# Attention logits from stacks of 48 float32r rows, two heads in the halves of TensorE's rows

## The chip, the cores and the metric

One core of one Trainium2 chip. The metric is the device time of one execution in microseconds; less is better. The kernel is one launch that does everything.

## The reference, cut to what matters

`x` is 2 x 2048 x 256 (batch, tokens, features). A layer norm with modulation from a condition vector gives `h`; then causal attention with 16 heads of 16 features, an output projection and a gated residual; then a second modulated norm, a two-layer net of 1024 hidden units with routed low-rank terms, and a second gated residual. The part at issue is the attention:

```python
qkv = x @ W_qkv.T + b_qkv
q, k, v = (heads(t) for t in jnp.split(qkv, 3, axis=2))     # n, 16 heads, 2048, 16
logits = jnp.einsum('bhqd,bhkd->bhqk', q, k) / jnp.sqrt(jnp.float32(HEAD))
logits = jnp.where(causal[None, None], logits, -jnp.inf)
attn = jax.nn.softmax(logits, axis=-1)
o = jnp.einsum('bhqk,bhkd->bhqd', attn, v)
```

## The kernel before, in words

There are three stages after a short set-up, each a block that all engines leave together.

**Stage 2, the projections** (to about 134 us). Eight blocks of 512 tokens: VectorE normalises, TensorE transposes and projects to q, k, v with each float32 operand split into a float32r high and low part, three passes (`product`, line 358). ScalarE copies q and k out twice (line 499): in float32 and as the first bfloat16 part. VectorE takes the rest (line 565) and the second part (line 567), POOL the third part (line 527); POOL also splits the weights of the last stage (lines 518, 522). SyncE stores the three parts to DRAM as `qk_parts`, four DMAs a block (line 425). ScalarE may not start block n before the store of block n - 2 has landed.

**Stage 3, the attention** (about 134 to 1067 us). Work goes by group: 4 heads (`GH`) of one batch, 8 groups. For each group, `kst` and `qst` hold 6 stacked rows-of-16 per head, the products of parts that are kept (1-1, 1-2, 1-3, 2-1, 2-2, 3-1), so that one bfloat16 matmul over 96 rows gives logits of about float32 quality; 6 DMAs for q and 6 for k bring one block of 512 tokens (lines 616 to 632). There are two passes over the logits:

- The pass for the maxima (`event`, line 711): logits with queries on the partitions, at most 512 columns in one of three PSUM banks (4 to 6), the causal mask of the diagonal added by a matmul of `mask_q` with a bfloat16 identity (lines 729, 732). VectorE reduces each bank to its row maximum (line 862) and so gives the bank back. When the last unit of a query block J is reduced, VectorE makes three bfloat16 parts of minus the maximum (`make_parts`, lines 835 to 845), TensorE turns them (line 720), VectorE copies them to `mT` (line 850), and three DMAs put them into rows 96 to 98 of `qst`. Rows 96 to 98 of `kst` are ones (POOL's memset, line 925). There are 140 units and 4 turns a group, 144 events.
- The pass for the sum (`logits`, line 743, and `values`, line 763): per tile of 128 keys (40 a group), logits over 99 rows with keys on the partitions (lines 756, 760), two heads to two PSUM banks; ScalarE's Exp of both banks (line 816); then the product with v, four heads at once in four groups of 32 array columns, in float32 (line 772), two tiles late. The probabilities' sum comes from a column of ones.

TensorE's order is written out by hand (lines 781 to 790). The events of the pass for the maxima run ahead: the first `AHEAD` = 69 events of the next group lie in the current group's tiles, and before the first group they run alone (line 777).

```python
                for n in range(NKT):
                    logits(n, 0)
                    maxima(SLOTS_OF_TILE * n)
                    if n >= PV_LAG:
                        values(n - PV_LAG, s, c)
                    ...
                    maxima(SLOTS_OF_TILE * n + 1)
                    logits(n, 1)
                    maxima(SLOTS_OF_TILE * n + 2)
```

The waits that tie the engines: an event waits for the reduction three banks earlier (line 716), `logits` for the Exp of the same half a tile earlier (line 754), `values` for the Exp of its tile (line 766). The groups' steps run in a loop of two (`over_steps`, line 876). After the last step TensorE does 24 matmuls that nobody reads (`UNREAD[0]`, line 794).

**Stage 4** (from about 1068 us) is the projection of the attention's output and the net; the diff does not touch it.

## Time and profile before

| | |
|---|---|
| runs | 1407.65, 1411.41, 1412.89 us (median 1411.41) |
| the profiled execution | 1412.92 us, its span 1411.2 us |
| TensorE busy (matmuls) | 1300.2 us (92%) |
| TensorE weight loads | 693.9 us (49%), beside the matmuls |
| VectorE busy | 1032.8 us (73%) |
| ScalarE busy | 774.5 us (55%) |
| POOL busy | 172.8 us (12%) |
| mean granted TensorE clock | 0.954 |

PE is TensorE's matmul, PEld its weight load, DVE VectorE, ACT ScalarE, SPq SyncE's DMA queue. A matmul's listed time includes the way through the array, so neighbours overlap; the distance from one start to the next is what one costs in a dense row. A clock of 1.00 is 2.4 GHz, 0.50 is 1.2 GHz.

### The profile page before, as it was taken

The numbers are of one execution on the slowest core, as the hardware profiler recorded it, in microseconds if no ns is written. First come the engines' busy times: TensorE is split into PE (matmuls) and PEld (weight loads), VectorE is DVE, ScalarE is ACT, GpSimd is POOL, SyncE is SP. The second block draws the span as 40 slices with busy tenths as digits, with TensorE's granted clock in tenths as the row PEclk, the third lists the DMA queues.
The fourth block names the chain that finished last, engine by engine and source line by source line (L and its number), as shares of the span: only waits on it lengthen the run. The fifth ranks groups of instructions, "written<-read, shape, count | busy, mean of one in ns | idle before, by whom it ended". The sixth has DMA issues, their size and how long they took to land. (4 is left out here: it accounts for less than half of the span.)

```text
span 1411.2 us, 26070 instructions
## 1 busy us (share of the span) xinstructions
PE 1300.2 (92%) x8566; PEld 693.9 (49%) x8566; DVE 1032.8 (73%) x1862; ACT 774.5 (55%) x1009; POOL 172.8 (12%) x101
## 2 busy tenths in 40 slices
PE   4983899999999999999998999999999899999997
PEld 3873233343333333333333334334326788888886
DVE  4893988888888778788787788888822566666663
ACT  2762046666666556566665666666681444454442
POOL 1468300000000000000000000000001212332221
PEclk8997589999999999999999999999999999999998
DMA  6444230021021011003003002000004001222200
GB/s 205 134 163 155 75 100 16 17 61 32 18 59 35 18 42 54 17 9 83 17 5 78 17 18 64 7 6 10 5 6 129 11 23 40 59 59 59 59 15 30
DMA packets 75813, 71.09 MB, mean 50 GB/s; under 512 B 17816, under 2 KB 68704, under 8 KB 75688
## 3 DMA queue, kind: packets, MB, share of 16 engines
q1 hardware_dynamic: 75688, 69.51, 17.9%
q8 instruction: 68, 1.11, 0.3%
q14 instruction: 57, 0.47, 0.1%
HBM read 47.57 MB, written 21.23 MB: 49 GB/s over the span
## 5 line engine op out<-in xcount | busy, mean ns | idle before, releaser
L862 DVE TENSOR_REDUCE mx<-ps 128x1 f32<-128x512 f32 (+3 forms) x1120 | 701.4, 671 | 152.5 <-PE ps L732 76.1
L816 ACT ACTIVATE prob<-ps 128x1024 f32<-128x1024 f32 (+3 forms) x640 | 547.8, 895 | 364.9 <-PE ps L760 222.1
L729 PE MATMUL ps<-kst,qst 96*128 96x512 bf16 (+3 forms) x1280 | 421.5, 362 | 25.0 <-DMA kst<-qk_parts 22.5
L756 PE MATMUL ps<-qst,kst 99*128 99x512 bf16 (+3 forms) x1280 | 358.8, 350 | 7.0 <-issue 6.1
L772 PE MATMUL ps<-prob,vw 128*32 128x512 f32 (+3 forms) x2560 | 300.6, 542 | 0.0
L729 PEld LDWEIGHTS ps<-kst,qst 96*128 96x128 bf16 x1280 | 121.4, 98 | 334.0 <-DVE mx L862 234.3
L756 PEld LDWEIGHTS ps<-qst,kst 99*128 99x128 bf16 x1280 | 119.2, 99 | 105.4 <-ACT prob L816 20.3
L760 PE MATMUL ps<-mask_k,ident_bf 128*128 128x128 bf16 x512 | 103.7, 222 | 0.0
L732 PE MATMUL ps<-mask_q,ident_bf 128*128 128x128 bf16 x512 | 102.9, 227 | 0.0
L772 PEld LDWEIGHTS ps<-prob,vw 128*32 128x32 f32 x2560 | 50.4, 108 | 105.3 <-issue 75.9
L935 POOL COPY vw<-v_nat 128x1024 f32 (+1 forms) x8 | 8.3, 1044 | 703.6 <-PE ps L772 703.5
L1327 DVE TENSOR_TENSOR hid_lo<-hidf,hid_hi 128x512 fp32r<-128x512 f32 x64 | 73.1, 1182 | 13.5 <-ACT hid_hi L1226 13.5
L1127 PE MATMUL ps<-w_hi,hid_hi 128*128 128x284 f32 x256 | 77.1, 323 | 1.9 <-ACT hid_hi L1226 1.9
L1127 PE MATMUL ps<-w_lo,hid_hi 128*128 128x284 f32 x256 | 75.2, 316 | 0.0
L1226 ACT ACTIVATE hidf<-ps,b_sb 128x512 f32<-128x512 f32 x64 | 43.9, 687 | 48.1 <-PE ps L1114 48.1
L362 PE MATMUL ps<-hT_hi,w_hi 128*128 128x512 f32 x128 | 53.0, 414 | 9.5 <-ACT hid_hi L1226 9.5
L760 PEld LDWEIGHTS ps<-mask_k,ident_bf 128*128 128x128 bf16 x512 | 51.0, 100 | 16.8 <-issue 0.8
L732 PEld LDWEIGHTS ps<-mask_q,ident_bf 128*128 128x128 bf16 x512 | 51.8, 101 | 9.8
L1127 PEld LDWEIGHTS ps<-w_hi,hid_hi 128*128 128x128 f32 x256 | 53.8, 210 | 3.9 <-ACT hid_hi L1226 3.6
L1127 PEld LDWEIGHTS ps<-w_lo,hid_hi 128*128 128x128 f32 x256 | 53.8, 210 | 0.4
L362 PE MATMUL ps<-hT_hi,w_lo 128*128 128x512 f32 x128 | 50.9, 397 | 0.0
L362 PE MATMUL ps<-hT_lo,w_hi 128*128 128x512 f32 x128 | 50.8, 397 | 0.0
(148 smaller groups left out, 1379.2 us busy)
## 6 DMA issues: line engine op xcount, KB each, us to landing
qk_parts<-parts SPq DMA_DIRECT2D x32, 384.0 KB, 3.0
qst<-qk_parts SPq DMA_DIRECT2D x192, 64.0 KB, 2.6
kst<-qk_parts SPq DMA_DIRECT2D x192, 64.0 KB, 2.5
xs<-in_x SPq DMA_DIRECT2D x16, 512.0 KB, 6.4
o_rows<-o_sb SPq DMA_DIRECT2D x128, 32.0 KB, 1.7
o_raw<-o_rows SPq DMA_DIRECT2D x16, 256.0 KB
rd<-rden_rows SPq DMA_DIRECT2D x16, 256.0 KB
out<-y SPq DMA_DIRECT2D x8, 512.0 KB, 3.2
```

Source lines behind the costliest of these rows:

```text
L362: last = pe.matmul(out, lhs(a, k), rhs(b, k), start=(start and k == 0 and n == 0), stop=(stop and k == chunks - 1 and n == len(PASSES) - 1))
L729: last = pe.matmul(at, qst[gc][0:QK_ROWS, J, h0 + h, i % 4 * P:(i % 4 + 1) * P], kst[gc][0:QK_ROWS, cb, h0 + h, 0:width], start=True, stop ...
L732: last = pe.matmul(at[:, width - P:width], ident_bf[:], mask_q[:], start=False, stop=True)
L756: last = pe.matmul(ps[:, h, 0:width], kst[c][0:ST_ROWS, t // 4, h, t % 4 * P:(t % 4 + 1) * P], qst[c][0:ST_ROWS, J, h, skip:BLK], start=Tr ...
L760: last = pe.matmul(ps[:, h, 0:P], ident_bf[:], mask_k[:], start=False, stop=True)
L772: last = pe.matmul(ps[32 * h:32 * h + 32, O_BANK, skip:BLK], vw[:, c, t, h, :], prob[:, n % P_BUFS, h, 0:BLK - skip], start=(t == 0), stop ...
L816: act.activation(prob[:, n % P_BUFS, 2 * pair:2 * pair + 2, 0:width], ps[:, 2 * pair:2 * pair + 2, 0:width], ACT.Exp).then_inc(exp_done, 1)
L862: dve.tensor_reduce(mx[:, h0:h0 + nh, i % 4, cb], ps[:, bank, 0:nh * width].rearrange("p (h x) -> p h x", h=nh), AX, ALU.max).then_inc(max ...
L935: pool.tensor_copy(vw[:, c, :, :, 0:HD], v_nat[:, c * nt:(c + 1) * nt, bass.ds(hs * (GH * HD), GH * HD)] .rearrange("p t (h d) -> p t h d" ...
L1127: last = pe.matmul(ps[:, Y_BANK + t, 0:D + ZP], hid[a][:, m, t * P:(t + 1) * P], w2_p[b][:, m, :], start=(e == 0), stop=(e == len(order) - 1))
L1226: act.activation(out, ps[:, H_BANK + m % 2, :], ACT.Relu, bias=b1_sb[:, m:m + 1]).then_inc(f1_out, 1)
L1327: dve.tensor_tensor(hid[1][:, m, :], hidf[:, m % HRING, :], hid[0][:, m, :].bitcast(F32), ALU.subtract).then_inc(hid_lo_done, 1)
```

## The change

Q and k are no longer split into three bfloat16 parts but into a float32r high and a float32r low part; the products high-high, high-low and low-high make 48 rows a head. Heads 2p and 2p + 1 lie in rows 0 to 47 and 64 to 111, each with two rows for the parts of the maximum behind it (rows 48, 49 and 112, 113). So each logits matmul uses one half of the array's rows, two heads go to two different banks, and an event of the maxima now fills two banks. The masks are added in two pieces of 64 rows each, four matmuls for two heads instead of two. `pick` holds shifted identities, `mask_k` and `mask_q` shifted masks. A group has now 73 units and 4 turns, 150 banks (118 reductions of 512 columns, 16 of 384 and 12 of 256), and the first 37 events, 72 banks, run ahead. The last slot of maxima in a tile is gone. `qk_rows` in DRAM is float32, stored by 12 DMAs a block (256 KB each) and loaded by 2 DMAs for q and 2 for k (192 KB each). POOL's third part and VectorE's second part in stage 2 fall away. The ones are written by two memsets on VectorE (first buffer) and two on POOL (second buffer) of 32 partitions x 4096 float32 each, before the first load of k. The diff, cut to its core:

```diff
-NPART = 3
-QK_ROWS = 6 * HD
-ST_ROWS = QK_ROWS + NPART
+ROWS = 3 * HD
+ST_ROWS = ROWS + 2
+NHP = GH // 2
...
-            for h in range(GH):
+            for p in range(NHP):
                 for c in range(J):
-                    units.append((J, i, h, 1, c, BLK, False))
-            together = {0: 4, 1: 2, 2: 1, 3: 1}[r]
-            for h in range(0, GH, together):
-                units.append((J, i, h, together, J, (r + 1) * P, True))
+                    units.append((J, i, slice(p, p + 1), c, BLK, False))
+            together = NHP if r == 0 or (r == 1 and J) else 1
+            for p in range(0, NHP, together):
+                units.append((J, i, slice(p, p + together), J, (r + 1) * P, True))
...
-T_LAG = 3
+T_LAG = 2
...
-NEV = len(EV)
+BANKS = [2 if kind == "logits" else 1 for kind, _ in EV]
+AT = [sum(BANKS[:e]) for e in range(len(EV) + 1)]
+NEV = AT[-1]
 assert NEV % S_BUFS == 0
-SLOTS_OF_TILE = 3
-AHEAD = 69
+SLOTS_OF_TILE = 2
+AHEAD = next(e for e in range(len(EV)) if AT[e] >= 72)
...
-    return [range(u * NEV // count, (u + 1) * NEV // count) for u in range(count)]
+    order = [*range(AHEAD, len(EV)), *range(AHEAD)]
+    slots, done = [[] for _ in range(count)], 0
+    for e in order:
+        slots[done * count // NEV].append(e)
+        done += BANKS[e]
+    return slots
...
-UNREAD = (24, 58, 40, 12)
+UNREAD = (32, 58, 40, 12)
...
-    qk_parts = nc.dram_tensor("qk_parts", [2, NPART, D, T], BF16, kind="Internal").ap()
+    qk_rows = nc.dram_tensor("qk_rows", [2, NH, ROWS, T], F32, kind="Internal").ap()
...
-        ident_bf = sb(whole, "ident_bf", [P, P], BF16)
-        mask_k = sb(whole, "mask_k", [P, P], BF16)
-        mask_q = sb(whole, "mask_q", [P, P], BF16)
+        pick = sb(whole, "pick", [P, 3, P], BF16)
+        mask_k = sb(whole, "mask_k", [P, 3, P], BF16)
+        mask_q = sb(whole, "mask_q", [P, 3, P], BF16)
...
+                for w in range(3):
+                    off = 64 * (w - 1)
+                    pool.affine_select(out=pick[:, w], in_=ones[:], compare_op=ALU.is_equal, fill=0.0, base=off,
                                        pattern=[[-1, P]], channel_multiplier=1).then_inc(pool0, 1)
-                pool.affine_select(out=mask_k[:], in_=zeros[:], compare_op=ALU.is_ge, fill=NEG, base=0,
-                                   pattern=[[1, P]], channel_multiplier=-1).then_inc(pool0, 1)
-                pool.affine_select(out=mask_q[:], in_=zeros[:], compare_op=ALU.is_ge, fill=NEG, base=0,
-                                   pattern=[[-1, P]], channel_multiplier=1).then_inc(pool0, 1)
...
-                    for c in range(2 * KC):
-                        if c % KC == 0:
-                            until(sp, part3_done, n * 2 + 1 + c // KC)
-                            alone(sp)
-                        dst = qk_parts[c // KC, :, c % KC * P:(c % KC + 1) * P, bass.ds(n * BLK, BLK)]
-                        sp.dma_start(dst.rearrange("a p t -> p a t"),
-                                     parts[:, q, :, c, :]).then_inc(parts_stored[q], 16)
+                    until(sp, low_done, n + 1)
+                    alone(sp)
+                    for w, lows in enumerate(((0, 0, 1), (0, 1, 0))):
+                        for c in range(KC):
+                            for slot, low in enumerate(lows):
+                                dst = qk_rows[w, 8 * c:8 * c + 8, slot * HD:(slot + 1) * HD, bass.ds(n * BLK, BLK)]
+                                sp.dma_start(dst, parts[low][:, q, KC * w + c, :].bitcast(F32)
+                                             ).then_inc(parts_stored[q], 16)
...
-                    until(pool, part2_done, n + 1)
-                    alone(pool)
-                    for cs in (slice(0, KC), slice(KC, 2 * KC)):
-                        pool.tensor_tensor(parts[:, q, 2, cs], rest[:, cs], parts[:, q, 1, cs],
-                                           ALU.subtract).then_inc(part3_done, 1)
...
-                    dve.tensor_tensor(rest[:], qkf[:], parts[:, q, 0], ALU.subtract).then_inc(rest1_done, 1)
-                    until(dve, rest1_done, n + 1)
-                    dve.tensor_copy(parts[:, q, 1], rest[:]).then_inc(part2_done, 1)
+                    dve.tensor_tensor(parts[1][:, q], qkf[:], parts[0][:, q].bitcast(F32),
+                                      ALU.subtract).then_inc(low_done, 1)
...
-        K_DMAS, Q_DMAS, O_DMAS = 6, 6, GH
+        K_DMAS, Q_DMAS, M_DMAS, O_DMAS = 2, 2, 2, GH
...
-            kst = [sb(tmp, f"kst{q}", [P, NJ, GH, BLK], BF16) for q in range(2)]
-            qst = [sb(tmp, f"qst{q}", [P, NJ, GH, BLK], BF16) for q in range(2)]
+            kst = [sb(tmp, f"kst{q}", [P, NJ, NHP, BLK], F32R) for q in range(2)]
+            qst = [sb(tmp, f"qst{q}", [P, NJ, NHP, BLK], F32R) for q in range(2)]
             vw = sb(tmp, "vw", [P, 2, S // P, GH, 2 * HD])
             prob = sb(tmp, "prob", [P, P_BUFS, GH, BLK])
-            mx = sb(tmp, "mx", [P, GH, 4, NJ])
-            negm = sb(tmp, "negm", [P, 2, GH * 4])
-            mparts = sb(tmp, "mparts", [P, NPART, GH * 4], BF16)
-            mT = sb(tmp, "mT", [NPART * GH * 4, NJ, P], BF16)
+            mx = sb(tmp, "mx", [P, 2, NHP, 4, NJ])
+            negm = sb(tmp, "negm", [P, GH * 4])
+            mparts = sb(tmp, "mparts", [P, 2, 2, NHP * 4])
+            mT = sb(tmp, "mT", [2 * GH * 4, NJ, P])
...
+            def load_rows(sp, w, dst, g, hg, J, loaded):
+                c = g % 2
+                for a in range(2):
+                    src = qk_rows[w].rearrange("(h a) r t -> a h r t", a=2)[
+                        a, bass.ds(hg * NHP, NHP), :, c * S + J * BLK:c * S + (J + 1) * BLK]
+                    sp.dma_start(dst[c][64 * a:64 * a + ROWS, J].bitcast(F32),
+                                 src.rearrange("h r t -> r h t")).then_inc(loaded[c][J], 16)
...
+                    def bank_of(b):
+                        at = AT[e] + b
+                        if not (isinstance(g, int) and g == 0 and at < S_BUFS):
+                            pe.wait_ge(max_red, g * NEV + at - S_BUFS + 1)
+                        return S_BANK + at % S_BUFS
...
-                    for h in range(nh):
-                        at = ps[:, bank, h * width:(h + 1) * width]
-                        last = pe.matmul(at, qst[gc][0:QK_ROWS, J, h0 + h, i % 4 * P:(i % 4 + 1) * P],
-                                         kst[gc][0:QK_ROWS, cb, h0 + h, 0:width], start=True, stop=not diagonal)
+                    def product_of(at, a, p):
+                        half = slice(64 * a, 64 * a + ROWS)
+                        return pe.matmul(at, qst[gc][half, J, p, i % 4 * P:(i % 4 + 1) * P],
+                                         kst[gc][half, cb, p, 0:width], start=True, stop=not diagonal)
+                    def mask_of(at, a, w):
+                        half = slice(64 * a, 64 * a + 64)
+                        return pe.matmul(at[:, width - P:width], pick[half, w - a + 1], mask_q[half, w - a + 1],
+                                         start=False, stop=(w == 1))
+                    bank = [bank_of(0), bank_of(1)]
+                    for p in range(pairs.start, pairs.stop):
+                        at = [ps[:, bank[a], (p - pairs.start) * width:(p - pairs.start + 1) * width] for a in range(2)]
+                        made = [product_of(at[a], a, p) for a in range(2)]
                         if diagonal:
-                            last = pe.matmul(at[:, width - P:width], ident_bf[:], mask_q[:],
-                                             start=False, stop=True)
-                    last.then_inc(max_mm, 1)
+                            for w in range(2):
+                                made = [mask_of(at[a], a, w) for a in range(2)]
+                        if p == pairs.stop - 1:
+                            for last in made:
+                                last.then_inc(max_mm, 1)
...
-                    for h in range(2 * pair, 2 * pair + 2):
-                        last = pe.matmul(ps[:, h, 0:width], kst[c][0:ST_ROWS, t // 4, h, t % 4 * P:(t % 4 + 1) * P],
-                                         qst[c][0:ST_ROWS, J, h, skip:BLK],
-                                         start=True, stop=(t < 4 * J))
-                        if t >= 4 * J:
-                            last = pe.matmul(ps[:, h, 0:P], ident_bf[:], mask_k[:], start=False, stop=True)
+                    for a in range(2):
+                        half = slice(64 * a, 64 * a + ST_ROWS)
+                        last = pe.matmul(ps[:, 2 * pair + a, 0:width],
+                                         kst[c][half, t // 4, pair, t % 4 * P:(t % 4 + 1) * P],
+                                         qst[c][half, J, pair, skip:BLK], start=True, stop=(t < 4 * J))
+                    if t >= 4 * J:
+                        for w, a in ((0, 0), (0, 1), (1, 0), (1, 1)):
+                            half = slice(64 * a, 64 * a + 64)
+                            last = pe.matmul(ps[:, 2 * pair + a, 0:P], pick[half, w - a + 1], mask_k[half, w - a + 1],
+                                             start=False, stop=(w == 1))
                     last.then_inc(st_done, 1)
...
                     maxima(SLOTS_OF_TILE * n + 1)
                     logits(n, 1)
-                maxima(SLOTS_OF_TILE * n + 2)
...
-                    m = negm[:, 0, :]
-                    link(dve.tensor_reduce(m.rearrange("p (h i) -> p h i", i=4), mx[:, :, :, 0:J + 1],
+                    link(dve.tensor_reduce(negm[:], mx[:, :, :, :, 0:J + 1].rearrange("p a h i c -> p (a h i) c"),
                                            AX, ALU.max, negate=True))
-                    link(dve.tensor_copy(mparts[:, 0, :], m))
-                    link(dve.tensor_tensor(negm[:, 1, :], m, mparts[:, 0, :], ALU.subtract))
-                    link(dve.tensor_copy(mparts[:, 1, :], negm[:, 1, :]))
-                    dve.tensor_tensor(mparts[:, 2, :], negm[:, 1, :], mparts[:, 1, :],
+                    m = negm[:].rearrange("p (a x) -> p a x", a=2)
+                    link(dve.tensor_copy(mparts[:, :, 0, :].bitcast(F32R), m))
+                    dve.tensor_tensor(mparts[:, :, 1, :].bitcast(F32R), m, mparts[:, :, 0, :],
                                       ALU.subtract).then_inc(m_parts, 1)
...
+                        for a in range(2):
+                            bank, nh = S_BANK + (AT[e] + a) % S_BUFS, pairs.stop - pairs.start
+                            if a:
+                                dve.wait_ge(max_mm, g * NEV + AT[e] + 2)
+                            dve.tensor_reduce(mx[:, a, pairs, i % 4, cb],
+                                              ps[:, bank, 0:nh * width].rearrange("p (h x) -> p h x", h=nh),
+                                              AX, ALU.max).then_inc(max_red, 1)
...
-                for J in range(NJ):
+                load_q(sp, 0, 0, 0)
+                sp.wait_ge(ones_set, 4)
+                load_k(sp, 0, 0, 0)
+                for J in range(1, NJ):
...
+                for a in range(2):
+                    dve.memset(kst[0][64 * a + 32:64 * a + 64].rearrange("p n h x -> p (n h x)").bitcast(F32),
+                               1.0).then_inc(ones_set, 1)
...
-                for q in range(2):
-                    pool.memset(kst[q][QK_ROWS:ST_ROWS], 1.0).then_inc(ones_set, 1)
-                pool.wait_ge(ones_set, 2)
+                for a in range(2):
+                    pool.memset(kst[1][64 * a + 32:64 * a + 64].rearrange("p n h x -> p (n h x)").bitcast(F32),
+                                1.0).then_inc(ones_set, 1)
+                pool.wait_ge(ones_set, 4)
```

## Rows read from the trace of the kernel before

**Rows 1.** Group by line and shape: busy us, mean ns; idle before.
```profile
L862 DVE TENSOR_REDUCE mx<-ps 128x1 f32<-128x512 f32 x896 | 574.6, 686 | 81.1 <-PE ps L729 70.1 <-PE ps L732 7.7
```

**Rows 2.** Busy time by stretch: start:end, length, then each engine's us, clock, DMA.
```profile
170.00:185.00 15.00, 14.22 (x38) 3.90 (x38) 15.00 (x27) 0.00 (x0) 0.00 (x0) 0.50 0.34 94
600.00:800.00 200.00, 193.55 (x1369) 73.62 (x1362) 165.42 (x292) 126.05 (x151) 2.08 (x2) 0.99 0.15 37
1040.00:1060.00 20.00, 19.81 (x134) 4.79 (x126) 0.00 (x0) 17.84 (x21) 0.00 (x0) 1.00 0.01 2
```

**Rows 3.** Timeline of POOL: start, us; one copy ends each group's step.
```profile
300.24 1.04 POOL L935 COPY vw<-v_nat 128x1024 f32 x1 [147.77 <-PE ps L772]
409.89 1.04 POOL L935 COPY vw<-v_nat 128x1024 f32 x1 [108.61 <-PE ps L772]
525.53 1.04 POOL L935 COPY vw<-v_nat 128x1024 f32 x1 [114.61 <-PE ps L772]
```

**Rows 4.** Timeline of TensorE over one full tile.
```profile
647.54 1.06 PE L772 MATMUL ps<-prob,vw 128*32 128x512 f32 x8
648.54 0.60 PE L729 MATMUL ps<-kst,qst 96*128 96x512 bf16 x2
648.98 0.60 PE L756 MATMUL ps<-qst,kst 99*128 99x512 bf16 x2
...
650.38 0.64 PE L772 MATMUL ps<-prob,vw 128*32 128x512 f32 x4
```

**Rows 5.** Timeline of TensorE at a diagonal tile of the same group.
```profile
641.24 0.22 PE L756 MATMUL ps<-qst,kst 99*128 99x128 bf16 x1
641.30 0.22 PE L760 MATMUL ps<-mask_k,ident_bf 128*128 128x128 bf16 x1
645.56 0.43 PE L772 MATMUL ps<-prob,vw 128*32 128x128 f32 x8
645.92 0.39 PE L729 MATMUL ps<-kst,qst 96*128 96x512 bf16 x1
```

**Rows 6.** Timelines of VectorE and ScalarE where each is the bound.
```profile
171.70 15.40 DVE L862 TENSOR_REDUCE mx<-ps 128x1 f32<-128x512 f32 x26
1041.41 3.90 ACT L816 ACTIVATE prob<-ps 128x1024 f32<-128x1024 f32 x4 [0.27 <-PE ps L756]
1062.18 0.58 ACT L807 COPY o_sb<-ps 128x512 f32<-128x512 f32 x1 [0.55 <-PE ps L772]
```

**Rows 7.** Timelines of float32r matmuls and a weight load in the other stages.
```profile
1200.00 0.40 PE L362 MATMUL ps<-hT_lo,w_hi 128*128 128x512 f32 x1
1200.23 0.40 PE L362 MATMUL ps<-hT_hi,w_lo 128*128 128x512 f32 x1
1177.14 0.26 PE L362 MATMUL ps<-ar_hi,hT_lo 128*128 128x28 f32 x1
1177.25 0.26 PE L362 MATMUL ps<-ar_hi,hT_hi 128*128 128x28 f32 x1
1200.23 0.19 PEld L362 LDWEIGHTS ps<-hT_hi,w_hi 128*128 128x128 f32 x1
```

**Rows 8.** Timelines of the end of stage 2 and the first matmul of stage 3.
```profile
119.57 0.73 ACT L499 ACTIVATE parts<-ps,bq_sb 128x512 bf16<-128x512 f32 x1
121.32 2.38 DVE L565 TENSOR_TENSOR rest<-qkf,parts 128x2048 f32<-128x2048 f32 x1 [4.52 <-POOL parts L527]
134.70 0.37 SPq L622 DMA_DIRECT2D qst<-qk_parts  x1
142.49 0.27 PE L729 MATMUL ps<-kst,qst 96*128 96x128 bf16 x1 [22.52 <-DMA kst<-qk_parts]
```

**Rows 9.** Groups by line and shape of two memsets.
```profile
L326 DVE MEMSET bl_sb<- 96x1024 f32 x1 | 0.9, 912 | 0.2 <-issue 0.2
L925 POOL MEMSET kst<- 3x8192 bf16 x2 | 13.8, 6919 | 4.2 <-POOLq L390 4.2
```

**Rows 10.** GB/s of the DMA queues from 100 to 135 us in 40 slices.
```profile
GB/s 351 387 314 0 0 0 0 0 0 19 0 323 358 218 135 376 379 9 0 0 0 0 7 365 380 356 384 306 9 0 0 0 0 123 376 384 358 384 173 0
```

93 lines of the change are left out of this document (39 added, 54 removed).

## The prediction, written before the changed kernel ran

> **What bounds the kernel now.** The page first, whose busy shares stand in the table above: TensorE 92% of the span, VectorE 73%, ScalarE 55%; most of VectorE's are the reductions, 896 of them of one bank of 512 columns, at 686 ns each [rows 1]. Busy shares mix stages, so next the stretches: from 600 to 800 us TensorE is busy 193.6 of 200 us at full clock, VectorE 165.4, ScalarE 126.1 [rows 2]. The attention stage is bound by TensorE, with VectorE not far behind. POOL's copies, one a group, give the step: 109.65 us, and 115.6 us for the next [rows 3]; the longer ones come once per round of the loop, and I let that extra stay.
>
> The timeline shows what a step is made of. A full tile takes 2.84 us: 1.00 us for the product with v and 1.84 us for eight logits matmuls of 512 columns, two of which take 0.44, so 0.22 each, and about 0.08 us for the way into the product with v, whose four heads lie in other columns of the array [rows 4]. A 128-column mask takes 0.06 us, the product with v at 128 columns 0.36 us [rows 5]. Summed over a group: 224 logits matmuls of 512 columns at 0.22 is 49.3; 96 narrower ones (384, 256, 128 columns) at 0.11 on average 10.6; 128 masks at 0.06, 7.7; products with v, 28 full tiles at 1.08 and twelve short ones (0.87, 0.65 and 0.44, by columns between the two rows), 38.1. Together 105.7 us of the measured 109.65, so the column count is the bound.
>
> VectorE behind it: 26 reductions of 512 columns back to back take 15.40 us, 0.592 each, in the stretch before the first group where VectorE is full and TensorE at half clock [rows 6, 2]. ScalarE's bound shows at the end, where no maxima are left: four Exps in 3.90 + 0.27 us [rows 6], 2.09 us a tile.
>
> **The change part by part.**
>
> *Two heads in the halves of the rows.* No float32r matmul on half the rows is in this trace. The nearest: a float32r matmul of 512 columns on all rows costs 0.23 us, against 0.22 in bfloat16, and those of 28 columns come 0.11 us apart, which is what one float32r weight load costs [rows 7]. A pair at best runs together: 0.23 us for 512 columns; for narrower ones its two weight loads bound it, 0.22. At worst the halves queue: 0.46. I take the good end, since the product with v shows four column strips working at once: four heads, float32, 512 columns in 1.00 us [rows 4], where a single bfloat16 one is 0.22 and float32r 0.23. A group has 160 pairs: 112 at 0.23 are 25.8 us, 48 at 0.22 are 10.6 us.
>
> *Masks in pieces.* 64 sets of four 128-column matmuls. Between two turns of 0.06 (halves together) and four (0.24); I take the middle, 0.18, since nothing shows a half-row bfloat16 load: 11.5 us instead of 7.7.
>
> *The product with v* stays, 38.1 us. TensorE's work a group: 25.8 + 10.6 + 11.5 + 38.1 = 86.0 us, 20 less than now.
>
> *VectorE.* 150 banks: 118 at 0.592 are 69.9; 16 of 384 and 12 of 256 columns, by columns with a fixed part, about 0.46 and 0.33, are 11.4; four turns with two fewer small operations, about 1.0 each. Together 85.3 us. So the next bound is at 85 to 86 us for two engines at once, and neither will reach it, because of what ties them.
>
> *Three banks, two an event.* An event now needs two free banks. TensorE gives one event before and one after the product with v. The chain: the event after v is issued; its first bank is complete 0.40 us later (a float32r matmul's listed time [rows 7]); VectorE reduces it, 0.69 with its latency [rows 1]; TensorE then issues the next event, 0.23, and stands until then, since this event is ahead of the product with v in its order. Then 0.08 and 1.00 for v, and the round closes: with 0.09 for two semaphores about 2.5 us a full tile, against VectorE's 2.23 on average and TensorE's 2.0. Twelve diagonal tiles have a shorter product with v, where VectorE (up to 4 x 0.592) closes last: 2.3. A step: 28 x 2.5 + 12 x 2.3 = 97.6, and 2 for turns. That is 99.5, 10 less than 109.65. The bounds: 86 (neither engine ever waits) and 107 (the rival on weight loads). Queued behind the waiting event are the product with v and the second logits pair; who waits for those is ScalarE, which has 1.95 us of work in 2.5 and so some cover. Seven steps: -70 us. The last step has no row at its start: 300.24 and six more steps, half at 109.65 and half at 115.6, come to 976, and it ends at 1062 us [rows 3, 6]; two thirds of it have maxima and gain in proportion, -5.5; the rest is ScalarE's and gives back only most of the 0.27, since two logits pairs now stand together: -1.5.
>
> *The events before the first group.* VectorE is full, 15.00 of 15 us, TensorE at 1.2 GHz [rows 2]. Columns to reduce are the same (72 of 150 banks). With two-bank events and the low clock the round of first bank, reduction, next event may take 1.3 instead of 1.19 us: +2 (0 to +7).
>
> *Stage 2.* POOL's third part, the second part's cast and a wait of 4.5 us go [rows 8]. The last block's parts would be ready some 2.4 us after ScalarE's last copy at 120.3, instead of after POOL's. But the stores double: 3.1 MB a block; at the 380 GB/s that the queues reach [rows 10] that is 8.3 us, with the load of x 9.7, about a block's own time. So the last store lands near 133 as it does now: -1 (-6 to +8). SyncE issues 12 stores instead of 4 a block; the load of x stands behind them, and if it came late all of stage 2 would follow.
>
> *Entry of stage 3.* The first load of k waits for four memsets. VectorE: 0.91 us for 1024 float32 a partition; POOL: 6.92 for 8192 [rows 9]. 4096 on either is 3.5 us, two of each at once 7 us. From 134.7 that is 141.8, then issue and landing of a load that is now two DMAs instead of six, to 145.5; now it is 142.5 [rows 8]. +3 (-2 to +6). Loads of later blocks have fewer DMAs on SyncE's queue; they were covered.
>
> *Small things.* UNREAD, the order of rows in mx, fewer DMAs for maxima: at nothing. The turn now has 32 rows instead of 48 and two small operations fewer before it.
>
> **The sum**: 1412.9 (the profiled execution) - 70 - 7 + 2 - 1 + 3 = 1340; the median of the runs is 1.5 lower, so **1338 us**.
>
> **The rivals.**
>
> *Weight loads are not hidden.* If a half cannot take its next weights while it works, a 512-column pair costs 0.11 + 0.23 = 0.34 us and a narrow one about 0.26, masks 0.24: 38 + 12.5 + 15.4 + 38.1 = 104, with today's 4 us of stalls 108 a step, 1.65 less than now; with the fixed terms **1403 us**. Against it: a load of float32r weights lies wholly under a matmul on the same 128 rows [rows 7]. The Trainium skill, TensorE: Matmul & The Clock Gate, The mechanism, states that a weight load overlaps running matmuls only if its row group differs, which would make this case. The trace contradicts it for full rows; for halves no row shows. 14%.
>
> *Slower: the halves queue.* One place, the pair of float32r matmuls. Each costs 0.23, the 128-column ones 0.11 instead of 0.06, and the doubled masks add 128 x 0.06 = 7.7: 105.7 + 2.2 + 1.6 + 7.7 = 117.2, step 121, +11.5 each; **1503 us** with the last step and the entry. It decides from 0.35 us a pair: (105.7 - 38.1 - 11.5) / 160. For it: the logits' halves write all 128 partitions of two banks at once, which the product with v never does. Against it: the four strips of v. 9%.
>
> *The clock falls.* TensorE will be busy about 80% in a step. In the last step the matmuls of a tile, 4 x 0.22 + 1.08 of 2.09 us, are 94%, and the clock is 1.00; in the stretch before, 512 columns at 1.2 GHz in 0.592 us are 72% and it stayed at 0.50 [rows 2, 6]. Between these nothing is shown. A step wholly at 1.2 GHz has 172 us of work; but then TensorE is full, which brought the clock back. A fifth of the time low would be +17 a step where it was 99.5, **1457 us**. 4%.
>
> *The change doesn't do what it says*, because an event has to wait for both reductions of the one before it (two engines in lockstep over three banks, for a reason that the waits in the code do not show): 0.59 more a full tile, 3.1 us, some 0.3 more in the others, a step of 116, +6.5: **1462 us**. Now the banks let VectorE lag by three events. 3%.
>
> **How the numbers follow.** A measurement here can tell about 0.5%, 7 us, from no change. Main case 70%, own range 1290 to 1375 (steps of 93 to 104.5 and the ends of the fixed terms). Weight loads 14%, half of it within 7 us; queueing halves 9%; clock 4%; lockstep 3%. Faster 0.70 + 0.07 = 0.77, same 0.07, slower 0.16. The range must hold 8 in 10: main case, stretched up to the weight-load rival's faster half, 1285 to 1400.
>
> **What would show it.** In the changed profile: matmuls of a pair starting 0.11 us or less apart and pairs 0.23 apart (else the first two rivals); a step of POOL's copies of 99.5 us; TensorE's waits on VectorE's reductions of some 0.4 us in each full tile, ahead of the product with v; VectorE busy 85% in the steps; PEclk near 1.00 there; first matmul of stage 3 near 145 us. A step below 92 us would say that the chain through three banks is not as I drew it, one above 107 that pairs cost over 0.33.

## The result, and the profile after

| | before | after |
|---|---|---|
| runs | 1407.65 to 1412.89, median 1411.41 us | 1523.69, 1525.02, 1532.34, median 1525.02 us |
| profiled execution, its span | 1412.92, 1411.2 us | 1523.69, 1522.0 us |
| TensorE busy | 1300.2 us (92%) | 1275.6 us (84%) |
| VectorE, ScalarE, POOL busy | 1032.8, 774.5, 172.8 us | 1020.2, 768.5, 126.6 us |
| mean granted TensorE clock | 0.954 | 0.879 |

The changed kernel is slower: ratio 1.0825, 95% interval 1.0762 to 1.0887. The prediction was 1338 us, faster; it was wrong in sign and outside its range. Medians and ratios here and below are of the fast runs: runs more than 1.5% above the fastest of their kernel stand outside them (three of the ten of e5_both, two of the eight of e7_single_twice, one of the six of e9_ones). Every engine in the table has less busy time than before, and all wait more. Where the 110.8 us between the two profiled executions lie, read from the first and last instruction of each stretch:

| stretch | before | after | difference | predicted |
|---|---|---|---|---|
| stage 2, to SyncE's first load of stage 3 | 134.7 | 182.5 | +47.8 | -1 |
| from there to the first matmul of the maxima | 7.8 | 12.7 | +4.9 | +3 |
| events before the first group | 43.5 | 59.7 | +16.2 | +2 |
| the eight groups, first logits to the last copy | 876.1 | 918.9 | +42.8 | -77 |
| stage 4 and the rest | 350.8 | 349.9 | -0.9 | 0 |

The page of after, the span in 40 slices of 38 us:

```profile
PE   4777046889889988989989989989989899999997
PEclk8978555999989889878999689998899999999999
```

PEclk is below 9 in many slices of the attention, where TensorE is busy 8 or 9 tenths. The other loss, in stage 2, shows in the DMA queues. From 100 to 135 us in 40 slices, the stretch of [rows 10]:

```profile
DMA  5555555555555995555555555555555555555555
GB/s 202 190 201 202 201 204 204 206 201 206 204 204 214 301 386 211 206 204 206 202 191 198 202 204 204 204 204 206 206 204 201 201 206 201 206 204 206 225 201 204
```

The queues never rest, and the 16 DMA engines are busy five tenths at some 204 GB/s; only where a block of x is loaded beside the stores (386) do they go faster. Before the change the same queues went up to 387 GB/s and stood still in between.

**Stage 2.** One block's stores by the queue's timeline, the stretch 50 to 80 us by windows (columns as in [rows 2]), and the longest waits from 20 to 182 us (total, times, longest):

```profile
153.69 2.28 SPq L439 DMA_DIRECT2D qk_rows<-parts_lo  x1
156.02 3.74 SPq L439 DMA_DIRECT2D qk_rows<-parts_hi  x3
159.81 1.08 SPq L439 DMA_DIRECT2D qk_rows<-parts_lo  x1
160.93 2.37 SPq L439 DMA_DIRECT2D qk_rows<-parts_hi  x2
```
```profile
50.00:80.00 30.00, 20.52 (x111) 17.92 (x110) 14.85 (x30) 14.97 (x26) 0.00 (x0) 0.83 0.58 207
```
```profile
ACT qkf L513 <- DMA qk_rows<-parts_hi: 49.4, 6, 10.9
DVE stats L382 <- DMA xs<-in_x: 36.8, 4, 11.7
```

A block now takes some 17 us (x is loaded at 92.25 and at 109.59 us), of which the 3.1 MB of stores at 204 GB/s need 15.4. ScalarE waits for the store of two blocks before; VectorE for x, whose load stands behind 12 stores on SyncE's queue.

**Entry** (timeline of all engines):

```profile
183.39 3.47 DVE L944 MEMSET kst<- 32x4096 f32 x1 [23.81 <-PEq L403]
187.77 3.47 DVE L944 MEMSET kst<- 32x4096 f32 x1 [0.91 <-issue]
191.27 0.79 SPq L628 DMA_DIRECT2D kst<-qk_rows  x2
195.21 0.48 PE L739 MATMUL ps<-kst,qst 48*128 48x128 f32 x2 [44.40 <-DMA kst<-qk_rows]
```

The memsets are 3.5 us each, as worked out; a start 0.91 us after the first load and a gap of 0.91 between the two make 1.8 of the 1.9 us over the forecast. [rows 8] has the same entry of before.

**Before the first group**, timelines of TensorE and VectorE:

```profile
237.32 0.80 PE L739 MATMUL ps<-kst,qst 48*128 48x512 f32 x2 [0.84 <-DVE mx L885]
238.96 0.47 PE L739 MATMUL ps<-kst,qst 48*128 48x128 f32 x2 [0.84 <-DVE mx L885]
```
```profile
238.12 1.29 DVE L885 TENSOR_REDUCE mx<-ps 128x1 f32<-128x512 f32 x2 [0.35 <-PE ps L739]
```

The pair is issued, both banks complete 0.80 later, VectorE takes 1.29 for the two, and the next event comes 1.64 after the last. In [rows 6] 26 reductions stood back to back; here VectorE has 0.35 of idle time in each round.

**The groups.** POOL's copies again give the steps (answers to [rows 3]), and the windows of the worst and of one of the best their clock:

```profile
374.25 1.04 POOL L965 COPY vw<-v_nat 128x1024 f32 x1 [179.06 <-PE ps L798]
486.48 1.04 POOL L965 COPY vw<-v_nat 128x1024 f32 x1 [111.18 <-PE ps L798]
607.26 1.04 POOL L965 COPY vw<-v_nat 128x1024 f32 x1 [119.74 <-PE ps L798]
732.43 1.04 POOL L965 COPY vw<-v_nat 128x1024 f32 x1 [124.14 <-PE ps L798]
847.52 1.04 POOL L965 COPY vw<-v_nat 128x1024 f32 x1 [114.04 <-PE ps L798]
965.55 1.04 POOL L965 COPY vw<-v_nat 128x1024 f32 x1 [116.99 <-PE ps L798]
```
```profile
607.00:732.00 125.00, 114.26 (x904) 46.58 (x900) 91.36 (x164) 68.64 (x84) 1.04 (x1) 0.80 0.09 23
732.00:847.00 115.00, 100.59 (x908) 41.75 (x900) 91.85 (x164) 69.98 (x86) 1.04 (x1) 0.94 0.20 44
```

The five steps are 112.2, 120.8, 125.2, 115.1 and 118.0 us, with 14, 30, 49, 14 and 30 us of them at 1.2 GHz (the granted clock summed over each step); before they were 109.7, 115.6, 110.5, 114.8 and 110.4 with 0, 7, 0, 3 and 0. Within either kind of step (they alternate with the loop of two), a microsecond at 1.2 GHz costs about 0.37: (125.2 - 112.2) / 35 and (120.8 - 115.1) / 16. The third step of the first kind agrees: 112.2 + 16 x 0.37 = 118.1. This slope is an estimate from five steps; put through the steps of all the kernels below at once it comes out at 0.37 to 0.38, with single steps off by up to 1.5 us. Without the low clock the steps would be some 107.0 and 109.9, about 3 less than before. Over all groups the low clock went from 14.5 to 185.9 us; 171 x 0.37 is +63, which leaves -21 for all else (seven steps of -3): the +42.8.

One full tile at full clock (answers to [rows 4]), and TensorE's longest total wait from 300 to 1150 us:

```profile
702.32 0.50 PE L739 MATMUL ps<-kst,qst 48*128 48x512 f32 x2
702.75 1.07 PE L798 MATMUL ps<-prob,vw 128*32 128x512 f32 x8
703.74 0.50 PE L739 MATMUL ps<-kst,qst 48*128 48x512 f32 x2
704.08 0.63 PE L779 MATMUL ps<-qst,kst 50*128 50x512 f32 x4
705.02 0.50 PE L739 MATMUL ps<-kst,qst 48*128 48x512 f32 x2 [0.31 <-DVE mx L885]
705.37 0.29 PE L744 MATMUL ps<-mask_q,pick 64*128 64x128 bf16 x4
```
```profile
PE ps L739 <- DVE mx L885: 65.9, 182, 1.9
```

Two matmuls on one line are a pair: their single records begin at 703.741 and 703.745, so the halves do work together. Two pairs back to back (704.08) begin 0.234 apart. A pair after a wait costs 0.34 to the next start: its weight loads lie bare. A tile here, from the event at 702.32 to the one at 705.02, is 2.70 us: 0.43 from the event to the product with v, 0.99 behind it, then 1.28 to the next event, which waits for the first bank's reduction.

### The profile page after: what moved, and what is told of

It is laid out like the page before. It is cut to its first block and busy times, and to the rows that moved or that the text cites. A ratio compares the mean times of both kernels' runs of the same rounds, so it can differ in the third digit from the quotient of the medians.

```text
span 1522.0 us, 27910 instructions
## 1 busy us (share of the span) xinstructions
PE 1275.6 (84%) x9598; PEld 724.6 (48%) x9598; DVE 1020.2 (67%) x1840; ACT 768.5 (50%) x1009; POOL 126.6 (8%) x91
## 5 line engine op out<-in xcount | busy, mean ns | idle before, releaser
L885 DVE TENSOR_REDUCE mx<-ps 128x1 f32<-128x512 f32 (+4 forms) x1168 | 708.9, 649 | 205.2 <-PE ps L744 102.3
L841 ACT ACTIVATE prob<-ps 128x1024 f32<-128x1024 f32 (+3 forms) x640 | 539.6, 894 | 433.3 <-PE ps L785 255.8
L739 PE MATMUL ps<-kst,qst 48*128 48x512 f32 (+3 forms) x1280 | 323.6, 504 | 150.1 <-DVE mx L885 100.0
L739 PEld LDWEIGHTS ps<-kst,qst 48*128 48x128 f32 x1280 | 137.8, 207 | 449.5 <-DVE mx L885 387.8
L798 PE MATMUL ps<-prob,vw 128*32 128x512 f32 (+3 forms) x2560 | 332.6, 595 | 0.1
L779 PE MATMUL ps<-qst,kst 50*128 50x512 f32 (+3 forms) x1280 | 243.8, 433 | 8.4 <-issue 6.2
L779 PEld LDWEIGHTS ps<-qst,kst 50*128 50x128 f32 x1280 | 130.3, 207 | 69.7 <-ACT prob L841 37.6
L744 PE MATMUL ps<-mask_q,pick 64*128 64x128 bf16 x1024 | 82.5, 244 | 0.0
L785 PE MATMUL ps<-mask_k,pick 64*128 64x128 bf16 x1024 | 76.8, 233 | 0.0
L513 ACT ACTIVATE qkf<-ps,bq_sb 128x512 f32<-128x512 f32 x32 | 22.2, 693 | 49.5 <-DMA qk_rows<-parts_hi 49.4
```

The source lines that it names most:

```text
L513: act.activation(out, ps[:, QK_BANK + c, :], ACT.Identity, bias=bq_sb[:, c:c + 1], scale=(HD ** -0.5 if c < KC else 1.0)).then_inc(qk_out, 1)
L739: return pe.matmul(at, qst[gc][half, J, p, i % 4 * P:(i % 4 + 1) * P], kst[gc][half, cb, p, 0:width], start=True, stop=not diagonal)
L744: return pe.matmul(at[:, width - P:width], pick[half, w - a + 1], mask_q[half, w - a + 1], start=False, stop=(w == 1))
L779: last = pe.matmul(ps[:, 2 * pair + a, 0:width], kst[c][half, t // 4, pair, t % 4 * P:(t % 4 + 1) * P], qst[c][half, J, pair, skip:BLK], s ...
L785: last = pe.matmul(ps[:, 2 * pair + a, 0:P], pick[half, w - a + 1], mask_k[half, w - a + 1], start=False, stop=(w == 1))
L798: last = pe.matmul(ps[32 * h:32 * h + 32, O_BANK, skip:BLK], vw[:, c, t, h, :], prob[:, n % P_BUFS, h, 0:BLK - skip], start=(t == 0), stop ...
```

## The experiments

All ratios are against runs of the kernel before on the same chip. "Low" is time at 1.2 GHz within the groups of the profiled execution (the recorded expectations count some 11 us more in every kernel). The profiled execution of e5_both is one of its longest, 1433.3 us, so its last column stands for a bad case.

| kernel | median us (runs) | ratio, 95% | first maxima matmul | before first group | groups, low |
|---|---|---|---|---|---|
| before | 1411.4 (3) | | 142.5 | 43.5 | 876.1, 15 |
| after | 1525.0 (3) | 1.0825, 1.0762 to 1.0887 | 195.2 | 59.7 | 918.9, 186 |
| e1_stores | 1458.2 (2) | 1.0340, 1.0279 to 1.0401 | 138.8 | 59.7 | 907.9, 151 |
| e2_split_waits | 1478.0 (2) | 1.0481, 1.0295 to 1.0667 | 196.8 | 42.9 | 878.6, 101 |
| e3_single | 1472.0 (2) | 1.0438, 1.0344 to 1.0532 | 197.7 | 42.9 | 876.8, 120 |
| e4_twice | 1501.7 (2) | 1.0649, 1.0595 to 1.0704 | 197.3 | 59.7 | 896.9, 99 |
| e5_both | 1413.1 (7) | 1.0066, 1.0026 to 1.0105 | 137.8 | 42.9 | 903.7, 170 |
| e6_both_twice | 1422.5 (6) | 1.0079, 1.0051 to 1.0107 | 139.1 | 42.9 | 889.3, 94 |
| e7_single_twice | 1400.3 (6) | 0.9933, 0.9895 to 0.9972 | 139.3 | 42.9 | 865.4, 67 |
| e8_single_stores | 1422.8 (4) | 1.0120, 1.0076 to 1.0163 | 140.3 | 42.9 | 884.2, 146 |
| e9_ones | 1385.8 (5) | 0.9829, 0.9808 to 0.9850 | 134.4 | 42.9 | 868.7, 72 |
| e10_v_bf16 | 1498.3 (1) | | 138.4 | 42.9 | 966.6, 967 |
| e11_order_twice | 1519.2 (1) | | 138.2 | 59.7 | 973.4, 173 |

**e1_stores: the stores' outermost dimension.** `dst` named 8 heads, then 16 rows. With the slots inside a head's row, head and row merge into one dimension of 128:

```diff
-"qk_rows", [2, NH, ROWS, T]
+"qk_rows", [2, NH, HD, 3, T]
-dst = qk_rows[w, 8 * c:8 * c + 8, slot * HD:(slot + 1) * HD, bass.ds(n * BLK, BLK)]
+dst = qk_rows[w, 8 * c:8 * c + 8, :, slot, bass.ds(n * BLK, BLK)].rearrange("h r t -> (h r) t")
```

The load's view of DRAM follows (`"(h a) r s t -> a h (r s) t"`); bytes and the number of DMAs stay.

> The changed kernel with one edit: rows of qk_rows in DRAM ordered (feature, slot) instead of (slot, feature), so that each store's destination is one run of 128 rows with one stride instead of 8 x 16. Bytes, DMAs and waits are the same. Theory A (a store whose outermost dimension is 8 keeps only half of the DMA engines busy: 204 GB/s at a share of 0.53 to 0.56 in the changed kernel): the queues go to some 370 GB/s, stage 3 starts near 138 us instead of 182.5, time near 1481 us. Rival B (the doubled bytes are simply too many, or writes do not go faster than 204 GB/s): stage 3 starts at 182 as before, time 1525 us.

The same stretch of stage 2 by windows, and the first load of stage 3 (the queue's timeline):

```profile
50.00:80.00 30.00, 29.31 (x173) 25.45 (x172) 23.88 (x49) 23.90 (x41) 0.04 (x1) 1.00 0.99 367
```
```profile
126.16 0.83 SPq L628 DMA_DIRECT2D qst<-qk_rows  x2
```

DMA share 0.99 and 367 GB/s, where the changed kernel had 0.58 and 207; TensorE is busy 29.3 of 30 us, and stage 3 starts at 126.2 us instead of 182.5. About half of the DMA engines' time had gone unused while the stores ran. The Trainium skill, DMA: Bandwidth & Descriptors, section "Why a DMA increments its semaphore by 16 and not by 1", says how many of the 16 engines a DMA gets: the largest number up to 16 that divides the slowest dimension's size on both sides. By that rule the old `dst` had 8 and the new one 16, and the trace agrees with both shares. Stage 2 without POOL's third part and the 4.5 us wait [rows 8] is then 8.5 us shorter than before. The gain of 67 us in the median is more than the 56 of the earlier start, and more than was expected: the groups took 11.0 us less, with 35 us less at the low clock (13 by the slope).

**e2_split_waits: each bank waits for itself.** The first matmul of a pair no longer waits for the second's bank:

```diff
-bank = [bank_of(0), bank_of(1)]
-for p in ...: made = [product_of(at[a], a, p) for a in range(2)]
+for a in range(2):
+    bank = bank_of(a)
+    for p in ...: last = product_of(at, a, p)
```

> The changed kernel with one edit: an event of the maxima waits for its first bank, does the first half's matmuls, and only then waits for the second bank. Theory A (an event that wants two free banks of three at once starves VectorE: 0.35 us of gap in every 1.64 us round before the first group): the stretch before the first group shrinks from 59.8 to about 45 us; the steps gain little (0 to 3 us of 118), because the second half, and the product with v behind it, still waits for the same reduction. Time near 1500 us. Rival B (the round is long because of TensorE's low clock and half-row matmuls, not because of the waits): the stretch stays at 57 to 60 us, time 1520 to 1530 us.

Before the first group 42.9 us instead of 59.7, all of what the change had lost there and 0.6 below the kernel before. The groups give 40.3 us, more than the 0 to 3 a step that were expected; by the slope above, 85 us less at the low clock are 31 of them.

**e3_single: one bank an event, three slots of maxima a tile**, as the kernel before had, in place of two banks and two slots:

```diff
-def event(g, gc, gh, e):
+def event(g, gc, gh, b):
+    e, a = BANK_EV[b]
...
-SLOTS_OF_TILE = 2
+SLOTS_OF_TILE = 3
```

> The changed kernel with the events of the maxima cut into single banks, each with its own wait, spread over three slots a tile (after the first logits, after the product with v, after the second logits), as the kernel before has them; two heads still lie in the halves of the rows, and the logits of the sum still run in pairs. Theory A (the steps are bound by the round event, reduction, event, product with v over three banks): TensorE has more to do, about 2.45 us of matmuls in a full tile, but no longer stands still; steps fall from 118 to 100 to 106 us, the stretch before the first group to 45 us, time 1410 to 1440 us. Rival B (the clock or the switching between array modes bounds the steps): steps stay above 112 us, time above 1480 us.

42.9 us and 876.8: the same as e2. The steps (108.9 to 115.6, where 100 to 106 were expected) and the time (1472.0 for 1410 to 1440) missed the theory. A full tile takes 2.70 us here too (products with v begin at 721.51, 724.21, 726.92). So the number of banks in an event costs 17 us before the first group, and of the 42.1 us in the groups the slope gives 24 to the clock (66 us less at 1.2 GHz) and leaves 18; but it does not set the full tile. What sets it here is not shown: TensorE is listed busy 8.81 of 9.00 us (719 to 728), and VectorE still has 0.2 to 0.3 us of idle time a tile.

**e4_twice: more work for TensorE.** In full tiles the second logits pair is computed twice into the same banks; results stay:

```diff
-for a in range(2):
+for a in [0, 1] * (1 + pair * (t < 4 * J)):
```

> The changed kernel with one edit: in full tiles the second pair of logits matmuls is done twice into the same banks (the second overwrites the first), 0.23 us more work on TensorE in a gap where it stands. Theory A (TensorE's clock falls to 1.2 GHz for about a fifth of the steps because it is less busy, and that costs some 8 us a step): the low time shrinks to less than half, steps fall from 118 to 110 to 113 us, time 1480 to 1500 us. Rival B (the clock's falls cost nothing, since VectorE and the banks set the pace): steps stay at 118 or grow by up to 5 us, time 1525 to 1560 us.

23 us faster with 0.23 us more work in every full tile, though the low clock fell to 99 us and not below half of 186. Timeline of TensorE:

```profile
643.13 1.06 PE L798 MATMUL ps<-prob,vw 128*32 128x512 f32 x8
644.12 0.50 PE L739 MATMUL ps<-kst,qst 48*128 48x512 f32 x2
644.46 0.87 PE L779 MATMUL ps<-qst,kst 50*128 50x512 f32 x6
645.40 0.50 PE L739 MATMUL ps<-kst,qst 48*128 48x512 f32 x2
645.84 1.06 PE L798 MATMUL ps<-prob,vw 128*32 128x512 f32 x8
```

The extra pair (x6 for x4) fell wholly into the wait: 644.12 to 645.40 is 1.28 again, and the tile 2.70. So the tile is no sum of TensorE's work. What the work brought was the clock: low 99 us for 186, which by the slope is 32 us; the groups gained 22.0. That leaves some 10 us as the price of the pairs, an estimate: with the low clock taken out e4's steps are 1 to 2 us longer. Where in a step that arises was not followed.

**e5_both and e6_both_twice** are e1 with e2, without and with the doubled pair.

> The changed kernel with the two edits of e1_stores (DRAM rows in the other order) and e2_split_waits (one wait for each bank) together. Theory (the two losses are separate: the stores' 56 us before stage 3; the two-bank waits' 17 us before the first group and some 40 us in the groups by way of gaps and clock): they add up, stage 3 starts near 126 us, the stretch before the first group is 43 us, the groups take about 877 us, time 1400 to 1412 us, no slower than the kernel before. Rival (part of e2's gain was the clock's chance): time above 1425 us.

> e5_both with the second pair of logits matmuls of each full tile done twice, as in e4_twice. Theory (the clock's falls to 1.2 GHz still cost in e5, about 0.3 us for each us of low clock, some 110 us of it in the groups): low time in the groups falls to 60 us or less, time 10 to 20 us under e5_both's. Rival (with the waits split there is no gap left that the extra matmuls fit into): time equal to e5_both's or up to 10 us above.

With both repairs the change is 0.7% slower than the kernel before, no longer 8%; the 1400 to 1412 us that were expected it missed. The ten runs of e5 spread from 1411 to 1441 us, a spread the kernel before does not have (1404 to 1414 in 21 runs). Doubling the pair narrowed it (1416 to 1427) but brought no gain: the ratios 1.0079 and 1.0066 can't be told apart, and e6 was expected 10 to 20 us under e5, with a low clock of 60 us or less. Here the clock theory got no support, and the rival (no gap is left that the extra matmuls fit into) held.

**e7_single_twice and e8_single_stores** are e1 with e3, with and without the doubled pair.

> e1_stores and e3_single together (single-bank events in three slots, better stores), with the second pair of logits matmuls of each full tile done twice. Theory (at full clock a full tile takes 2.70 us in every variant, because three banks of reductions, 1.78 us, do not cover the time between the last event before the product with v and the first after it with VectorE's start: the pace is VectorE's 4 x 0.59 us and a gap of 0.3): like e6_both_twice within 10 us, full tiles at 2.7 us. Rival (the single events were held back by the clock alone): full tiles at 2.5 us or less and steps of 100 us.

> e7_single_twice without the repeated logits matmuls: better stores and single-bank events in three slots. Theory (the clock's falls cost some 0.3 us for each us of low clock, and the repeated matmuls hold them off): low time in the groups above e7's 78 us, time 5 to 20 us above e7's 1405. Rival (e7's gain over e5 came from the single events, not from the clock): time within 5 us of e7's, or below.

The clearest test of the clock: the two differ by the doubled pair alone. The one with more work is 22 us faster (1400.3 and 1422.8, with ratios of 0.9933 and 1.0120 to their own runs of before, whose intervals do not meet), low 67 us and 146. The profiled groups differ by 18.8 us; the slope gives 29 for the clock and leaves 10 as the price of the pairs, as in e4. Windows of e7, and TensorE's timeline at the two gaps:

```profile
485.00:505.00 20.00, 17.15 (x161) 8.90 (x157) 15.39 (x26) 10.37 (x14) 0.00 (x0) 1.00 0.09 23
505.00:532.00 27.00, 26.03 (x161) 13.24 (x163) 14.64 (x26) 11.37 (x15) 1.04 (x1) 0.51 0.36 75
540.00:660.00 120.00, 117.12 (x1074) 62.10 (x1070) 101.86 (x184) 78.28 (x96) 1.04 (x1) 1.00 0.16 37
```
```profile
505.97 0.80 PE L775 MATMUL ps<-qst,kst 50*128 50x512 f32 x2 [3.76 <-issue]
731.48 0.80 PE L775 MATMUL ps<-qst,kst 50*128 50x512 f32 x2 [3.50 <-issue]
```

Once a round of the loop TensorE waits for nothing that the profile shows, for 3.5 to 3.8 us; from there the clock is 0.51 for 27 us, though TensorE is busy 26.0 of 27. Away from that, from 540 to 660 us, it is 1.00. The kernel before has such gaps too (2.98 us before 519.09 and 3.14 before 745.39), but only 7 and 3 us at 1.2 GHz around their ends; the windows of the first:

```profile
518.00:525.00 7.00, 5.91 (x30) 2.42 (x34) 1.81 (x3) 2.35 (x3) 0.00 (x0) 0.52 0.41 106
525.00:530.00 5.00, 5.00 (x46) 2.36 (x50) 4.72 (x8) 3.26 (x6) 1.04 (x1) 1.00 0.50 137
```

**e9_ones: the ones in another order.** e7, and the first buffer's ones are written by VectorE and POOL at once, so that the first load of k waits for one memset of each:

```diff
-for a in range(2):
-    dve.memset(kst[0][64 * a + 32:64 * a + 64]..., 1.0).then_inc(ones_set, 1)
+for q in range(2):
+    dve.memset(kst[q][32:64]..., 1.0).then_inc((ones_first, ones_set)[q], 1)
...
-sp.wait_ge(ones_set, 4)
+sp.wait_ge(ones_first, 2)
```

POOL does the same for `kst[q][96:128]`; the second buffer's loads wait for `ones_set`.

> e7_single_twice with the memsets of ones reordered: VectorE and POOL each write one half of the first kst buffer, then one half of the second, and the first load of k waits for the first two only. Theory (the entry of stage 3, 12.7 us against 7.8 before, is the serial memsets): first matmul of stage 3 some 4 us earlier against the start of the stage, time 1398 to 1403 us against e7's 1405. Rival (the load of k is late for another reason): no change.

Timeline of the entry:

```profile
126.90 3.47 DVE L944 MEMSET kst<- 32x4096 f32 x1 [9.41 <-PEq L400]
130.40 0.79 SPq L626 DMA_DIRECT2D kst<-qk_rows  x2
131.18 3.47 DVE L944 MEMSET kst<- 32x4096 f32 x1 [0.80 <-issue]
134.42 0.44 PE L738 MATMUL ps<-kst,qst 48*128 48x128 f32 x1 [21.29 <-DMA kst<-qk_rows]
```

The load goes out behind the first memset, and maxima begin at 134.4 us. This kernel, 1385.8 us, ratio 0.9829 (0.9808 to 0.9850), is 1.7% faster than the kernel before. It is 14.5 us below e7, whose runs were made on another chip. The entry explains about 5 of them (first maxima matmul 134.4 for 139.3), and the two profiled executions are only 3.5 us apart (1393.7 and 1397.2); the rest is more than this edit can be shown to do, and the runs of both spread (1389 to 1429, 1383 to 1412).

**e10_v_bf16: less work in the product with v.** e8, with `prob` and `vw` in bfloat16 (a less exact product with v):

```diff
-vw = sb(tmp, "vw", [P, 2, S // P, GH, 2 * HD])
-prob = sb(tmp, "prob", [P, P_BUFS, GH, BLK])
+vw = sb(tmp, "vw", [P, 2, S // P, GH, 2 * HD], BF16)
+prob = sb(tmp, "prob", [P, P_BUFS, GH, BLK], BF16)
```

> e8_single_stores with probabilities and v kept in bfloat16, so that the product with v is a bfloat16 one (a less exact computation) and takes about a quarter of the streaming time. Theory (three banks of reductions do not cover the product with v and the exposed weight loads around it, hence 2.70 us a full tile): with the product down from 1.0 us to about 0.35 the gap of VectorE goes, and a full tile with four banks of 512 columns takes 2.38 to 2.45 us at full clock, VectorE without a gap. Rival (VectorE's own latency between banks, or the array's mode switches, set the 2.70): full tiles stay at 2.6 to 2.7.

It was meant for the tile of 2.70 us and can't say anything of it, since no tile ran at full clock. Its page, and a window in the groups:

```profile
PE   4993999999999999999999999999999899999997
PEclk8995555555555555555555555555555999999999
```
```profile
600.00:800.00 200.00, 195.51 (x1182) 123.23 (x1181) 147.11 (x264) 114.43 (x133) 1.04 (x1) 0.50 0.10 25
```

TensorE is busy 195.5 of 200 us, and the clock is 1.2 GHz in all 966.6 us of the groups: 75 us slower than e8 (one run), for less work. A full TensorE did not bring the clock back.

**e11_order_twice: the chain of the full tile.** e1 with e4's doubled pair, and another order in the tile:

```diff
 logits(n, 0)
-maxima(SLOTS_OF_TILE * n)
 values(n - PV_LAG, s, c)
-maxima(SLOTS_OF_TILE * n + 1)
+maxima(SLOTS_OF_TILE * n)
 logits(n, 1)
+maxima(SLOTS_OF_TILE * n + 1)
```

> Edit: the layout of e1_stores and the doubled second logits pair of e4_twice, and in a tile the order logits, values, maxima, logits (twice), maxima in place of logits, maxima, values, maxima, logits (twice). Nothing else, so TensorE's work in a tile is that of e4_twice. Theory, the chain of the three banks: the loop from one event's start over its first bank, that bank's reduction and the next event is 1.28 us (read in the changed kernel: 703.74 to 705.02), and the product with v costs it 0.43 us from the event's start to its own and 0.99 behind, 1.42 in all; a full tile is 1.42 + 1.28 = 2.70. With the new order the way from the second event over the first logits pair (0.34), into the product with v (0.43) and out (0.99) is 1.76, and the other loop stays 1.28: a full tile of 3.04 us at full clock, a step some 8 to 12 us longer than e4_twice's clock-free 107.8. Rival, the 2.70 us is TensorE's work or VectorE's four reductions with their gaps, whatever the order: 2.70 again, steps within 2 us of e4_twice's at equal clock. Second rival: VectorE's reductions of both banks stand for the loop (2 x 0.615 + 0.1): then the order matters little, 2.7 to 2.8.

Timeline of TensorE:

```profile
631.05 0.50 PE L739 MATMUL ps<-kst,qst 48*128 48x512 f32 x2
631.39 0.63 PE L779 MATMUL ps<-qst,kst 50*128 50x512 f32 x4
632.34 0.50 PE L739 MATMUL ps<-kst,qst 48*128 48x512 f32 x2 [0.32 <-DVE mx L885]
632.68 0.40 PE L779 MATMUL ps<-qst,kst 50*128 50x512 f32 x2
633.01 1.06 PE L798 MATMUL ps<-prob,vw 128*32 128x512 f32 x8
634.00 0.50 PE L739 MATMUL ps<-kst,qst 48*128 48x512 f32 x2
```

From event to event 1.29 us, then 1.66 over the logits and the product with v: 2.95, where 3.04 was expected (v begins 0.33 after the logits, not 0.43) and the rivals said 2.70 to 2.8. The groups take 973.4 us, 76.5 more than e4's; 74 us more at the low clock are 27 of them, and with that taken out the steps are 5 to 7 us longer, less than the 8 to 12 expected, as a tile of 2.95 for 3.04 would have it. With the same work and another order the tile changed as the chain says, so the chain is shown, for events of two banks.

## Why the prediction was wrong, point by point

**Stage 2: -1 (-6 to +8), measured +47.8.** Of the 184 us between the sum (1340) and the profiled execution, this is 49. The step that failed is "at the 380 GB/s that the queues reach": it took the rate of the old stores for new ones of another shape. The old had 128 partitions outermost, the new 8 heads, and ran at some 204 GB/s. The text saw that the load of x stands behind 12 stores and that all of stage 2 would follow if it came late, and gave that 8 us. The access pattern was in the diff. With the stores at full rate (e1: 367 GB/s) the forecast's direction would have held: -8.5.

**Events before the first group: +2 (0 to +7), measured +16.2.** The round of bank, reduction and next event was put at 1.3 us against 1.19 for two reductions; it measured 1.64. Both reductions stand in it, 1.29, and 0.35 of idle time, because the pair starts only when both its banks are free and so leaves VectorE one bank. Undone by e2 and by e3 alone.

**The groups: -77, measured +42.8.** Three parts.
- *The pairs were right*: 0.23 each, halves together. The rivals "the halves queue" (9%) and "weight loads are not hidden" (14%) both fell. The sentence of the Trainium skill that the second leaned on (TensorE: Matmul & The Clock Gate, The mechanism: a weight load overlaps running matmuls only if its row group differs) is contradicted for halves as well: at 703.85 the loads for line 779 begin, while line 739's pair, begun at 703.74, works on the same rows. What the Trainium skill says on the same page, section Measured speedup vs the span model, that each further tile packed into the array adds about 4 ns, agrees with the pair's starts at 703.741 and 703.745. A set of four masks took 0.10 us to a following logits pair (701.38 to 701.48) and 0.22 into the product with v (705.37 to 705.59), against 0.18.
- *"About 2.5 us a full tile" was 2.70.* This is the second step that failed. The chain was the right one (e4, e11) with one link too short: each event after a wait bares its float32r weight loads, 0.10 on the way to the first bank (0.50 instead of 0.40), and 0.12 on the way into the product with v (0.43 instead of 0.23 + 0.08). 0.2 us in each of the 40 tiles are 8 us a step, and the clock-free step came out at 107.0 instead of 99.5, 56 us over all groups (-21 for -77). That the twelve diagonal tiles lose the same is taken from the sum; single ones were not followed.
- *The clock.* The third step that failed, and the dearest: +63 us where the sum had nothing. The rival "the clock falls" had 4% and a price of +17 a step for a fifth of the time; a fifth of the groups (186 of 919 us) ran at 1.2 GHz, at 0.37 per microsecond, some 9 us a step. Its share of the time was near and its price twice too high; what failed is the chance, and the sentence that a full TensorE brings the clock back, which e10 refutes for this work. Neither row it rested on (a stretch that stayed at 0.50, one that was at 1.00) had half-row matmuls.

**Entry: +3, measured +4.9**, in its bounds. **Lockstep** (3%) happened only before the first group. **The sum**: by these terms, with the clock as before and the stores at full rate, the change would have come out some 8 us faster, 0.6%: -8.5 + 4.9 + 16.2 - 21, an estimate. No run shows that case alone.

## What to carry to other kernels

Read the outermost dimension of each new DMA's two sides before you take a rate from an old one: 8 instead of 128 cost 56 us of stage 2 here, with all else the same. Where a change takes work off the engine that bounds, count the chain that is left link by link, with weight loads that a wait lays bare, and look at the granted clock of each step, not of the page alone: the cycles saved can be lost again at half speed. An event that needs two buffers out of three is close to lockstep; give each buffer its own wait.

## What the runs showed of the hardware that was not expected

- More TensorE work made kernels faster: 23 us with a pair done twice (e4), 22 us in e7 against e8, each with less time at 1.2 GHz. In e6 against e5 it did not.
- With the product with v in bfloat16 the clock stayed at 1.2 GHz for 966.6 us of attention, TensorE busy 98% of it. After a gap of 3.8 us e7, with half rows, stayed low for 27 us at 96% busy; the kernel before, with full rows, was low for 7 us at a gap of 3.0. That half-filled rows are the reason is a guess; no run varied the rows alone.
- Stores with 8 outermost ran at some 204 GB/s with the DMA engines five tenths busy; with 128 outermost the same stretch (50 to 80 us, x included) went from 207 GB/s and 0.58 to 367 and 0.99.
